# A gated cross-attention layer with 128 experts: half of the experts' output features computed with exchanged operands and carried through DRAM, and a gather of the routing by two 64-row tiles

## What is computed

```python
x = x + tanh(g_xattn) * attention(layernorm(x), ctx, ctx, Wq, Wk, Wv, Wo, bo)
x = x + tanh(g_ffn)   * ffn(layernorm(x), controller, f1, bias, f2)

def ffn(x, controller, f1, bias, f2):              # 32 experts x 4 sets = 128 slots
    grouped = x.reshape(4, 16, 32, 256)            # 64 groups of 32 tokens
    logits = einsum('bgtd,des->bgtes', grouped, controller) + tie
    perm = (logits == logits.max over the 32 tokens)          # one token a slot and group
    dispatched = einsum('bgtd,bgtes->bgesd', grouped, perm)
    inner = relu(einsum('bgesd,desf->bgesf', dispatched, f1) + bias)
    intermediate = einsum('bgesf,esfd->bgesd', inner, f2)
    return einsum('bgesd,bgtes->bgtd', intermediate, perm)
```

## Time and profile before

| | us |
|---|---|
| median of three runs (lowest, highest) | 292.98 (292.14, 294.31) |
| the profiled execution | 291.55 |
| span of its profile | 289.8 |
| PE busy | 239.9 (83%) |
| DVE busy | 204.4 (71%) |
| ACT busy | 172.6 (60%) |
| POOL busy | 128.8 (44%) |

### The profile page before, as it was taken

The page is one execution under the profiler, slowest core; times in us unless marked ns, Lnnn a source line. Parts: engine busy times, 40 slices in busy tenths (PEclk is TensorE's granted clock), DMA queues, the critical chain, the costliest instruction groups (busy, mean ns, idle before and its releaser), DMA issues.

```text
span 289.8 us, 7624 instructions
## 1 busy us (share of the span) xinstructions
PE 239.9 (83%) x2914; PEld 190.6 (66%) x2914; DVE 204.4 (71%) x446; ACT 172.6 (60%) x361; POOL 128.8 (44%) x243
## 2 busy tenths in 40 slices
PE   0638495997897997979988878589998999989995
PEld 0527393776675876867766655467776888877773
DVE  4985758599996895957777799899995555522222
ACT  3433667577587686855766646267775545455552
POOL 5652445647776678762756656525544000000000
PEclk9996869799999999998999999999999999999999
DMA  7855679442434342242200000089910000001222
GB/s 204 192 149 147 183 187 267 115 113 58 133 104 129 96 112 78 74 129 58 56 4 6 4 4 1 12 308 392 387 67 2 1 2 2 2 20 60 69 72 72
DMA packets 27237, 29.52 MB, mean 102 GB/s; under 512 B 3459, under 2 KB 22595, under 8 KB 27203
## 3 DMA queue, kind: packets, MB, share of 16 engines
q1 hardware_dynamic: 26771, 28.46, 33.1%
q10 hardware_dynamic: 432, 0.59, 0.9%
HBM read 14.06 MB, written 2.10 MB: 56 GB/s over the span
## 4 chain that ended last, share of the span: by engine, by line
PE 31%; DVE 20%; POOL 20%; issue 17%; ACT 5%; SPq 3%; DMA 3%; ACTq 0%; POOLq 0%; DVEq 0%
POOL pT L410 8%; PE banks L817 8%; PE banks L789 6%; PE banks L771 6%; PE banks L826 3%; DVE rsum L1155 3%; PE banks L526 2%; SPq L269 2%; DVE permb L1200 2%; POOL xs L404 2%; POOL qp L387 2%; POOL onl L434 2%; DMA w<-in_wattn_dram 2%; DVE xn L1100 2%; PE banks L635 2%
## 5 line engine op out<-in xcount | busy, mean ns | idle before, releaser
L1147 DVE TENSOR_REDUCE nmax<-banks 128x4 f32<-128x512 f32 x64 | 43.7, 683 | 29.3 <-PE banks L589 29.3
L410 POOL TENSOR_SCALAR_AFFINE_SELECT pT<-pT 128x512 f32<-128x512 f32 x64 | 41.0, 642 | 47.2 <-ACT pT L917 47.1
L922 ACT ACTIVATE banks<-cb 128x512 f32<-128x512 bf16 x62 | 37.0, 596 | 9.8 <-DVE nmax L1147 9.7
L917 ACT ACTIVATE pT<-banks 128x512 f32<-128x512 f32 x64 | 37.5, 589 | 8.8 <-PE banks L606 8.3
L606 PE MATMUL banks<-qst,kst 99*128 99x128 bf16 x256 | 25.9, 225 | 4.3 <-DMA qst<-nT 3.6
L635 PE MATMUL banks<-pT,va 128*32 128x128 f32 x512 | 27.7, 289 | 0.8 <-POOL pT L410 0.8
L1155 DVE RECIPROCAL rsum<-banks 128x256 f32<-128x256 f32 x16 | 28.0, 1747 | 0.0
L589 PE MATMUL banks<-kst,qst 96*128 96x128 bf16 x256 | 26.2, 227 | 1.9 <-ACT banks L922 1.6
L635 PE MATMUL banks<-pT,ones 128*32 128x128 f32 x512 | 26.2, 277 | 0.0
L1042 ACT ACTIVATE ys<-banks 128x1024 f32<-128x1024 f32 x16 | 16.7, 1047 | 14.3 <-PE banks L817 14.2
L1334 DVE SCALAR_TENSOR_TENSOR xs<-banks,tg,xs 128x256 f32<-128x256 f32 x16 | 7.7, 484 | 24.5 <-PE banks L826 24.5
(11 more groups left out here) (120 smaller groups left out, 643.3 us busy)
## 6 DMA issues: line engine op xcount, KB each, us to landing
wx<-in_wexp_dram SPq DMA_DIRECT2D x32, 256.5 KB, 7.3
kst<-kp SPq DMA_DIRECT2D x48, 128.0 KB, 2.5
qst<-qp SPq DMA_DIRECT2D x48, 128.0 KB, 2.4
cT<-in_ctxT_dram SPq DMA_DIRECT2D x8, 256.0 KB, 3.5
out_dram<-xs SPq DMA_DIRECT2D x16, 128.0 KB, 1.7
xs<-in_x_dram SPq DMA_DIRECT2D x3, 512.0 KB, 4.1
xs<-in_x_dram SPq DMA_DIRECT2D x2, 256.0 KB, 3.8
w<-in_wattn_dram ACTq DMA_DIRECT2D x2, 256.0 KB, 5.0
```

The source lines that it names most:

```text
L410: pool.affine_select(p, p, [[0, HC], [1, P]], ALU.is_ge, 0.0, base=0, channel_multiplier=-1)\
L917: act.activation(pT[:, n % PR, :], BT[n % 2], ACT.Exp, scale=float(D) ** -0.5).then_inc(p_ready, 1)
L922: act.activation(BS[n % 2], causal, ACT.Copy).then_inc(mask_placed, 1)
L1147: dve.tensor_reduce(nmax[:, b % 2, :].rearrange("p (e j o) -> p e o j", e=2, o=KH)[:, e, o], BS[n % 2].rearrange("p (j t) -> p j t", j=HC) ...
```

## The change

It changes routing, experts and combine.

Routing: the gather uses two row tiles of 64 tokens, each with its two groups. `permb` holds two copies instead of four, masked by the parity of the group (`parity`, now made during attention), so it has 256 columns; one of the gather's matmuls has 64 rows and 256 columns, and there are eight a block instead of four. The logits with their ramp stay in PSUM (`tied`), and the comparison writes `permT` directly, so `pc` and POOL's copy are gone. The high part of the rows, `rh`, is written by POOL from the fourth block on, no more by ACT. The slots are numbered anew (`ctrl_sb` is made with two copies).

Experts: they are taken in another order (`ORDER`, also that of the loads), in which each two consecutive pairs use four experts whose 16 slots stand eight apart. For the second half of the features the output is computed as before. For the first half the operands are exchanged: `hb` is stationary and the weights move, so that groups, not features, stand on the output's partitions. `keep_y` has two copies of 256 columns on each engine instead of one of 512; the first fills `sent`, four buffers used in turn. SP writes each pair's `sent` to `y_rows` in DRAM with two transfers (128 KB each, pieces of 512 bytes), and for every second pair it reads 16 slots back into 16 partitions of `big` (512 KB, 32 KB for each partition).

Combine: only the second half of the features is transposed (four transposes a block), into four banks, for eight blocks ahead of the first `combine`; ACT and DVE copy them in turn, over what was the first half of `routed`. `combine` reads the rows from DRAM and the transposed ones as one operand.

```diff
+ORDER = tuple(p // 4 + (0, 8, 4, 12)[p % 4] + e for p in range(PAIRS) for e in (0, PAIRS))
+YR = 4
+EARLY_Y = 8
...
+        permb = routing.enter_context(nc.sbuf_tensor("permb", [P, 2, 2, P], F32R))
+        routing.close()
+        big = sb("big", [P, 1 + KH, SLOTS * GROUPS])
         wx = sb("wx", [P, NE, KH * P + E + 1])
-        routed = sb("routed", [P, KH, SLOTS, GROUPS])
-        permb = sb("permb", [P, 2, NG, P], F32R)
-        ys = sb("ys", [P, 2, NG, E])
-        by_set = routed[:, :, :, :].rearrange("p h (t c e) g -> p t h c (e g)", t=2, c=2)
+        routed = big[:, 1:].rearrange("p h (s g) -> p h s g", g=GROUPS)
+        by_set = routed[:, KH - 1].rearrange("p (c t e) g -> p t c e g", c=2, t=2)
+        ys = big[:, 1, :].rearrange("p (b x) -> p b x", b=NB)
+        y_rows = nc.dram_tensor("y_rows", (SLOTS, GROUPS, P), F32).ap()
+        sent = [xn[:, 2 * i:2 * i + 2, :] for i in range(2)] + [t[:, :, :, :].rearrange("p a h s -> p a (h s)") for t in (rp, ctrl2)]
...
+            def load_rows(p):
+
+                for i in (p, p + 1):
+                    sp.wait_ge(y_sent[i % YR], 2 * 16 * (i // YR + 1))
+                e = ORDER[2 * p]
+                sp.dma_start(big[e::8, 0, :], y_rows[e::8].rearrange("s g j -> s (g j)")).then_inc(y_loaded, 16)
+
+            for p in range(PAIRS):
+
+                sp.wait_ge(y_kept_act, p + 1)
+                sp.wait_ge(y_kept_dve, p + 1)
+                for c in range(2):
+                    at = c * HALF + ORDER[2 * p]
+                    sp.dma_start(y_rows[at:at + 3 * PAIRS + 1:PAIRS].rearrange("x g j -> g x j"),
+                                 sent[p % YR][c * HALF:(c + 1) * HALF].rearrange("g t (e j) -> g (t e) j", e=2))\
+                        .then_inc(y_sent[p % YR], 16)
+                if p % 2 == 1 and p >= 3:
+                    load_rows(p - 3)
+            load_rows(PAIRS - 2)
...
-            def keep_perm(b, k):
-
-                pool.wait_ge(perm_ready, b + 1)
-                pool.tensor_copy(permT[:, b, :], pc[:, k, :]).then_inc(permT_kept, 1)
+            def rows_high(b):
+                pool.wait_ge(rn_ready, b + 1)
+                if b >= 4:
+
+                    pool.wait_ge(d_done, b - 3)
+                pool.tensor_copy(rh[:, b % 4], xn[:, b % 4]).then_inc(rh_ready, 1)
...
-                keep_perm(b, b % 2)
                 if b + 3 < NB:
+                    rows_high(b + 3)
                     split_rows(b + 3, (b + 3) % 4)
-                if b == 4:
-
-                    pool.wait_ge(consts_loaded, 16)
-                    pool.tensor_tensor(parity[:, :], groupmask[:, 0:2], groupmask[:, 2:4], ALU.add).then_inc(parity_step, 1)
-                    pool.wait_ge(parity_step, 1)
...
-                        last = pe.matmul(BD[k][h][:, :], part[:, b % 4, h * P:(h + 1) * P],
-                                         permb[:, k, :, :].rearrange("p g s -> p (g s)"), start=(q == 0), stop=(q == 1))
+                        for t in range(2):
+                            rows = slice(t * HALF, (t + 1) * HALF)
+                            last = pe.matmul(BD[k][t][:, h * E:(h + 1) * E], part[rows, b % 4, h * P:(h + 1) * P],
+                                             permb[rows, k, :, :].rearrange("p g s -> p (g s)"),
+                                             start=(q == 0), stop=(q == 1), tile_position=(t * HALF, 0),
+                                             skip_group_check=True)
...
-                for e in (2 * p, 2 * p + 1):
-                    for h in range(KH):
-                        for t in range(2):
-                            to = bank[4 + 2 * (p % 2) + t].rearrange("p (h c e g) -> p h c e g", h=KH, c=2, e=2)
-                            last = pe.matmul(to[:, h, :, e % 2, :],
-                                             wx[t * HALF:(t + 1) * HALF, e, KH * P + h * P:KH * P + (h + 1) * P],
-                                             hb[t * HALF:(t + 1) * HALF, e % HR, :, :], start=True, stop=True,
-                                             tile_position=(t * HALF, 0), skip_group_check=True)
+                for i in (2 * p, 2 * p + 1):
+                    e = ORDER[i]
+                    for t in range(2):
+                        to = bank[4 + 2 * (p % 2) + t]
+                        f = slice(t * HALF, (t + 1) * HALF)
+
+                        pe.matmul(to[:, 0:E].rearrange("p (c e g) -> p c e g", c=2, e=2)[:, :, i % 2, :],
+                                  wx[f, e, KH * P + P:KH * P + E], hb[f, i % HR, :, :], start=True, stop=True,
+                                  tile_position=(t * HALF, 0), skip_group_check=True)
+
+                        last = pe.matmul(to[:, E + (i % 2) * P:E + (i % 2 + 1) * P],
+                                         hb[f, i % HR, :, :].rearrange("p c g -> p (c g)"),
+                                         wx[f, e, KH * P:KH * P + P], start=True, stop=True,
+                                         tile_position=(t * HALF, 0), skip_group_check=True)
...
-            BY2, BC = (bank[4:6], bank[6:8]), bank[0:2]
+            BY, BC = bank[4:8], bank[0:2]
 
             def transpose_y(b):
-                k = b % 2
-                if b >= 2:
-
-                    pe.wait_ge(ys_ready, b - 1)
+                if b >= 4:
+
+                    pe.wait_ge(ys_ready[b % 2], (b - 4) // 2 + 1)
                 for g in range(NG):
-                    for h in range(KH):
-                        o = (g % 2) * E + h * P
-                        last = pe.transpose(BY2[k][g // 2][:, o:o + P], routed[:, h, :, b * NG + g], ident)
+                    last = pe.transpose(BY[b % 4][:, g * P:(g + 1) * P], routed[:, KH - 1, :, b * NG + g], ident)
                 last.then_inc(yT_done, 1)
 
             def combine(b):
                 k = b % 2
-                pe.wait_ge(ys_ready, b + 1)
+                pe.wait_ge(ys_ready[k], b // 2 + 1)
                 if b >= 2:
                     pe.wait_ge(yo_ready, b - 1)
                 for g in range(NG):
-                    last = pe.matmul(BC[k][g * T:(g + 1) * T, 0:E], permT[:, b, g * T:(g + 1) * T],
-                                     ys[:, k, g, :], start=True, stop=True, tile_position=(0, g * T))
+                    at = (b * NG + g) * P
+                    last = pe.matmul(BC[k][g * T:(g + 1) * T, 0:E].rearrange("p (h j) -> p h j", h=KH),
+                                     permT[:, b, g * T:(g + 1) * T], big[:, 0:2, at:at + P], start=True, stop=True,
+                                     tile_position=(0, g * T))
                 last.then_inc(c_done, 1)
 
             pe.wait_ge(y_kept_act, PAIRS)
             pe.wait_ge(y_kept_dve, PAIRS)
-            pe.wait_ge(permT_kept, NB)
-            transpose_y(0)
+            for b in range(EARLY_Y):
+                transpose_y(b)
+            pe.wait_ge(y_loaded, 16 * PAIRS // 2)
             for b in range(NB):
-                if b < NB - 1:
-                    transpose_y(b + 1)
                 combine(b)
+                if b + EARLY_Y < NB:
+                    transpose_y(b + EARLY_Y)
...
+                for t in range(halves):
+                    last = act.activation(routed[:, :, :, b * NG + 2 * t:b * NG + 2 * t + 2],
+                                          bank[5 - 2 * (b % 2) + t][:, :].rearrange("p (h g s) -> p h s g", h=KH, g=2),
+                                          ACT.Copy)
...
                 act.wait_ge(e_done, p + 1)
-                act.activation(by_set[:, 0, :, :, 2 * p * GROUPS:2 * (p + 1) * GROUPS],
-                               bank[4 + 2 * (p % 2)].rearrange("p (h c x) -> p h c x", h=KH, c=2), ACT.Copy)\
+                if p >= YR:
+
+                    act.wait_ge(y_sent[p % YR], 2 * 16 * (p // YR))
+                act.activation(sent[p % YR][:, 0, :], bank[4 + 2 * (p % 2)][:, E:], ACT.Copy)
+                act.activation(by_set[:, 0, :, ORDER[2 * p]:ORDER[2 * p + 1] + 1:PAIRS, :],
+                               bank[4 + 2 * (p % 2)][:, 0:E].rearrange("p (c e g) -> p c e g", c=2, e=2), ACT.Copy)\
                     .then_inc(y_kept_act, 1)
...
+            def tied(b):
+
+                return bank[3 if b == 1 else (2, 7)[b % 2]][:, P:2 * P]
 
             def add_ramp(b):
+                if b < 2:
+
+                    dve.wait_ge(p_ready, CH - 1 + b)
+
+                dve.wait_ge(lg_done, b + 1)
+                dve.tensor_tensor(tied(b), bank[1][:, 0:P], tie, ALU.add).then_inc(lt_ready, 1)
+
+            def pick(b):
+
+                lg = tied(b).rearrange("p (g t) -> p g t", g=NG)
                 if b > 0:
-
                     dve.wait_ge(perm_ready, b)
-
-                dve.wait_ge(lg_done, b + 1)
-                dve.tensor_tensor(lt[:, :], bank[1][:, 0:P], tie, ALU.add).then_inc(lt_ready, 1)
-
-            def pick(b):
-
                 dve.wait_ge(lt_ready, b + 1)
                 dve.tensor_reduce(gmax[:, :], lg, AX_X, ALU.max).then_inc(gmax_ready, 1)
                 dve.wait_ge(gmax_ready, b + 1)
```

(20 more changed lines are left out.)

110 lines of the change are left out of this document (56 added, 54 removed).

## The result

The changed kernel takes 285.12 us in the median of four runs (283.67 to 286.56); the kernel before, on the same chip, 293.44 (292.14 to 294.31). The ratio is 0.972 (95% interval 0.9655 to 0.9785). The forecast was 281.2 in a range of 274.5 to 288.5.

A forecast was written before the change was run, and what follows sets the result against it. PE was taken to bound experts and combine, with PE, DVE and ACT all near full in routing. Terms -7.0 + 0.4 + 3.5 + 0.15 - 8.8 = -11.75 took 291.55 to 279.8; plus 1.4 for the median, 281.2 us, range 274.5 to 288.5.

The forecast's parts named there:

- Routing, -7.0: Routing stage: blocks take 1.6 us instead of 2.13, so 7.0 us less, bounds -8.4 and -2.9.
- PE at 1.40: Routing: PE's work per block after the change, with the new gather's eight instructions at about 0.58 us.
- Rival 2: Routing: POOL and DVE exclude each other, 2.0 us a block, 4 us less gain, total 285.3; chance 0.13.
- Experts, +3.65: Experts stage: +3.5 us for the order of row tiles and +0.15 for the last pair's copies.
- the middle answer: `expert_out`: matmuls start in program order, five slots of 0.22 us instead of four, +0.22 a pair, +3.5 in all.
- rival 1: `expert_out`: row tiles are served independently, so their order costs nothing; total 277.7 us; chance 0.13.
- Rows from DRAM, 7.3: Between experts and combine: rows are in SBUF 7.3 us after the last copy, bounds 5.8 and 10.
- Combine, -8.8: From the last copy to the end: 25.6 us instead of 34.4, so -8.8, bounds -10.3 and -6.1.
- up to 2 us more: Combine: PE's idle time might lower its clock, costing up to 2 us more.
- a gap over 5 us: Sign that the forecast is wrong: PE idle over 5 us between 32 transposes and first combine; about 2 expected.
- Attention's end, +0.4: End of attention: POOL's extra work on `parity` and `ctrl_sb` adds 0.4 us, bounds 0 and +0.7.
- rival 3: `expert_out`: tile 1 can't load weights meanwhile, or nothing overlaps: up to +14.2 us, total 284 to 292; chance 0.17.

The follow-up runs named there:

- routing_only: The kernel before with only the routing part of the change, experts and combine as before: 287.81 us, ratio 0.9808.
- wide_gather: The changed kernel with the gather back to 128 rows, four masks and 512 columns: 291.49 us, ratio 0.9918.
- rh_act: The changed kernel with the cast to `rh` back on ACT: 286.62 us, ratio 0.9768.
- lt_sbuf: The changed kernel with logits and ramp summed into a buffer in SBUF again and compared from there: 286.31 us, ratio 0.9723.
- alt_tiles: The changed kernel with the four `expert_out` matmuls of an expert over row tiles 0, 1, 0, 1 instead of 0, 0, 1, 1: 283.07 us, ratio 0.9593.
- no_dram: The changed kernel without transfers through DRAM, combining a plane already in SBUF, so half the output features are not the experts': 278.31 us, ratio 0.9444.
- padded: The changed kernel with each slot's rows 34 KB apart in DRAM instead of 32: 283.56 us in one execution.
- early16: The changed kernel with all 16 blocks transposed before PE waits for the rows from DRAM, instead of 8: 278.20 us, ratio 0.9455.

## Why the prediction was right, and where its terms were not

**Routing, -7.0: right in sum, and partly by luck.** From first gather to first `expert_in` it was -7.1 in `routing_only`, and -5.8 in the profiled execution, where the clock's drop was longer. Against the second profile of before, `routing_only` has -6.3: the prediction's 2.13 us a block before was read from one profile, and in the other it is 2.02. The period was forecast as 1.6 and is 1.64. But the engine was another: the prediction had PE at 1.40 and took 1.6 as a round-up over several loops, while PE alone is 0.67 + 0.64 + 0.22 + 0.11 = 1.64. The mis-sized terms are PE's: the gather 0.58 against 0.67, and the rest 0.82 against 0.97. `wide_gather`, `rh_act` and `lt_sbuf` price the parts at 4.7, about 1.6 and at most 1.6 us; together they are more than 7, for each run puts one part back while the others stay, and another engine may then set the pace.

**Rival 2, POOL and DVE excluding each other, is half right.** `normalize` goes from 0.40 to 0.61 and, with the cast on ACT, back to 0.40. Beside POOL's subtraction it ends 0.16 behind it, much as the comparison did in the earlier trace rows (0.14); the prediction had taken that 0.14 as a sign against the rival. It costs nothing here, because PE sets the pace of 1.64. In `wide_gather`, where DVE sets it, single ones take up to 0.81. The rival's 2.0 us a block needed `normalize` to wait for cast and subtraction, and the next cast for `normalize`; in the rows quoted the cast is over (206.64) before `normalize` starts (206.99), and only the last 0.46 us of the subtraction are waited out. The Trainium skill (SBUF — State Buffer, "Who interferes with whom") has a `tensor_scalar` between SBUF tensors among those that can contend with GpSimd, and here the trace agrees (0.62 against 0.40).

**Experts, +3.65: too much by 2.0.** A pair takes 2.22, not 2.33. The step that failed is the middle answer, matmuls starting strictly in program order, which the prediction backed by a row of the trace and by the Trainium skill (TensorE: Matmul & The Clock Gate, "The mechanism"). The trace of the changed kernel disagrees: PE begins the other tile's matmul ahead of one that waits. The truth lies between the answer and rival 1: the order costs one slot of 0.11 a pair and not two. That every start before stood in program order proved nothing, since there tiles alternated and nobody had to wait. That exchanging the operands costs nothing was right (`alt_tiles`: 2.11 a pair, before 1.02 + 1.09), and so was that no `keep_y` waits for a transfer: without any transfers, in `no_dram`, the stage is as long.

**Rows from DRAM, 7.3: they took 10.2**, just over the bound. Two issues were to start at the last copy; SP was still at the writes of the pair before (issued from 253.67), 1.2 us late (254.49 to 255.69). The last write landed 3.3 us after its issue and not 1.7 to 2.5, the read 5.0 and not 4.1 with 0.4 for the one before it. Of the 2.9 us missing, 1.2 are SP's lateness, 1.2 the write and 0.5 the read. The two landings were borrowed from other transfers. The lateness was left out: the copies of the last two pairs end only 0.9 us apart (253.61 and 254.49), and the two issues between take 1.9. Why these writes and reads land later than the borrowed ones stays open. The pitch in DRAM is not it: `padded` lands no earlier. As an estimate, the Trainium skill (DMA: Bandwidth & Descriptors, "Latency and other measured facts", 207 GB/s at a pitch of 512 KB) would have put about 1.1 us more on the read; no run here shows such a cost of the pitch.

**Combine, -8.8: it was -4.1.** 2.9 of the 4.7 us are the rows, 1.3 the clock, which the prediction had as "up to 2 us more" and left out of its sum, and 0.5 the rest. The forecast named a gap over 5 us as the sign that it is wrong; the gap was 5.2. So by its own sign the combine's part failed, though the total held. The mis-sized term is the 7.3 us for the rows, and the clock was put at nothing in the sum. Here the runs also show what was not forecast: 32 more transposes stood ready to fill the gap, and with them the combine is 7.1 us shorter (`early16`).

**Attention's end, +0.4: nothing.** The stretch from POOL's extra work to the first gather is no longer than before where the clock did not fall. The 2.8 us of the table lie almost wholly ahead of that work.

**The sum.** By the profiled execution 2.8 + 1.2 - 2.0 + 4.7 = 6.7 us were missing, of which the clock in attention and routing holds up to 4. The median is 1.4 below that execution, and the prediction had put 1.4 on top for the median of before: 6.7 - 2.8 = 3.9. It stayed in the range because the experts' 2.0 us offset part of it, and because the range was wide enough to take in half of rival 3. That the total is near is in part luck: four terms are off by 1 to 5 us and have different signs.

## What to carry to other kernels

A transfer at the end of a stage costs its issue behind everything queued before it, its own measured landing and, if the engine that waits falls idle, perhaps the clock afterwards; so keep as much independent work as the wait is long, and place it there (7 us here by one constant). When several banks come free, spend them on the loop that runs through them (2.8 us here). And before pricing a stage, compare like with like: the first gather came between 188.0 and 191.7 us in traces with nearly the same attention, and one stage of one unchanged kernel took 33.2 us in one profile and 32.3 in the next.
